# A feed-forward whose gate and up projections use seven block products for each eight, two batches at a time

## What is computed

```python
def _L0_ffn_ref(h_shard, w_gate_up, w_down):          # INTER = 2048
    gate_up = jnp.einsum('bsh,oh->bso', h_shard, w_gate_up)
    gate, up = jnp.split(gate_up, 2, axis=-1)
    h = jax.nn.silu(gate) * up
    return jnp.einsum('bsi,hi->bsh', h, w_down)
...
x = x + _L0_attn_a_ref(_layernorm(x, axis=-1), ...)
x = x + _L0_ffn_ref(_layernorm(x, axis=-1), L0_ffn_w_gate_up, L0_ffn_w_down)
x = x + _L0_attn_b_ref(_layernorm(x, axis=-1), ...)
x = x + _L0_ffn_ref(_layernorm(x, axis=-1), L0_ffn_w_gate_up, L0_ffn_w_down)
```

## Time and profile before

| | us |
|---|---|
| median of 3 runs | 3209.04 (3207.11 to 3210.09) |
| the profiled execution, whole | 3208.35 |
| its span, first to last instruction | 3207.1 |
| TensorE busy in the span | 3056.9 (95%) |
| VectorE, ScalarE, GpSimd busy | 2126.6, 1530.9, 584.5 |
| granted TensorE clock, mean of the span | 0.978 of full speed |

### The profile page before, as it was taken

How to read it: one execution, slowest core, us unless ns; L and a number is a source line. 1 busy time by engine, 2 the same in 40 slices (tenths; PEclk the granted TensorE clock), 3 DMA queues, 4 the chain that set the end, 5 groups by cost and what they waited for, 6 DMA issues and landing times.

```text
span 3207.1 us, 44240 instructions
## 1 busy us (share of the span) xinstructions
PE 3056.9 (95%) x17041; PEld 1739.5 (54%) x17041; DVE 2126.6 (66%) x4092; ACT 1530.9 (48%) x2483; POOL 584.5 (18%) x429
## 2 busy tenths in 40 slices
PE   6999999999999799999799999989899888999999
PEld 3434334334333344444488888854344336888887
DVE  6998998998989777776444334446676766444343
ACT  4988888888888366666511111014343342111110
POOL 1000000000000445442100001004454451001000
PEclk9999999999999799999899999999999988999999
DMA  2000000000000000000110000043232312001001
GB/s 74 2 1 11 1 1 11 1 1 11 1 1 2 1 2 1 2 1 2 59 40 20 20 20 1 1 131 86 66 99 79 86 34 79 20 20 40 1 1 53
DMA packets 32855, 86.96 MB, mean 27 GB/s; under 512 B 7235, under 2 KB 7236, under 8 KB 30469
## 3 DMA queue, kind: packets, MB, share of 16 engines
q1 hardware_dynamic: 30022, 83.43, 8.8%
q10 hardware_dynamic: 2624, 0.69, 0.1%
HBM read 59.60 MB, written 20.97 MB: 25 GB/s over the span
## 4 chain that ended last, share of the span: by engine, by line
PE 43%; DVE 3%; DMA 2%; POOL 2%; issue 1%; ACT 1%; SPq 0%; ACTq 0%; POOLq 0%; DVEq 0%
PE ps L1201 22%; PE ps L1215 11%; PE ps L1578 3%; POOL ex_sum L1546 2%; PE ps L1642 1%; PE ps L1608 1%; PE ps L1566 1%; PE ps L1619 1%; PE ps L1593 1%; DMA k_stack<-halves 1%; DMA halves<-lo_b 1%; DVE out_t L1706 1%; DVE ffn_z L1227 1%; PE ps L1186 1%; DVE sums_sb L1705 0%
## 5 line engine op out<-in xcount | busy, mean ns | idle before, releaser
L655 DVE TENSOR_SCALAR pair_in<-key_words,row_words 128x512 f32<-128x512 f32 x1792 | 726.1, 480 | 44.2 <-PE ps L542 40.2
L740 ACT ACTIVATE pair_mid<-ps,row_bias 128x512 f32<-128x512 f32 x896 | 588.2, 688 | 133.2 <-PE ps L542 115.8
L542 PE MATMUL ps<-pair_in,w_hi 128*64 128x512 f16 x3584 | 584.3, 390 | 8.6 <-DVE pair_in L655 8.2
L1278 ACT ACTIVATE ffn_silu<-ps 128x512 f32<-128x512 f32 x128 | 76.2, 595 | 831.4 <-PE ps L1201 831.4
L1240 DVE TENSOR_TENSOR ffn_inner<-ffn_silu,ps 128x512 f32<-128x512 f32 x128 | 87.9, 687 | 550.5 <-PE ps L1201 550.5
L542 PEld LDWEIGHTS ps<-pair_in,w_hi 128*64 128x64 f16 x3584 | 202.2, 108 | 301.6 <-issue 66.8
L1003 DVE TENSOR_REDUCE maxes<-ps 128x2 f32<-128x1024 f32 x256 | 303.1, 1221 | 93.6 <-PE ps L919 92.5
L542 PE MATMUL ps<-pair_in,w_lo 128*64 128x512 f16 x1792 | 352.1, 388 | 0.0
L1047 ACT ACTIVATE ex<-ps 128x512 f32<-128x512 f32 x448 | 243.2, 595 | 118.9 <-PE ps L938 118.4
L1201 PE MATMUL ps<-ffn_z_hi,ffn_w_hi 128*128 128x512 f32 x1024 | 277.4, 393 | 1.7 <-ACT ffn_w_hi L1267 1.7
L1201 PE MATMUL ps<-ffn_z_hi,ffn_w_lo 128*128 128x512 f32 x1024 | 274.7, 390 | 1.9 <-POOL ffn_w_lo L1285 1.9
(11 more groups left out here) (209 smaller groups left out, 4420.0 us busy)
## 6 DMA issues: line engine op xcount, KB each, us to landing
ffn_raw<-in_w_ffn SPq DMA_DIRECT2D x14, 1536.0 KB, 6.7
q_stack<-halves SPq DMA_DIRECT2D x48, 256.0 KB, 5.1
k_stack<-halves SPq DMA_DIRECT2D x48, 256.0 KB, 5.9
halves<-hi_b SPq DMA_DIRECT2D x16, 512.0 KB, 2.6
halves<-lo_b SPq DMA_DIRECT2D x16, 512.0 KB, 3.6
out<-x SPq DMA_DIRECT2D x4, 1024.0 KB, 4.3
x<-in_x SPq DMA_DIRECT2D x6, 512.0 KB, 5.9
ffn_raw<-in_w_ffn SPq DMA_DIRECT2D x6, 512.0 KB, 4.7
```

The costliest lines, as they stand in the source:

```text
L542: s = nc.tensor.matmul(ps[F2 * half:F2 * half + F2, bank + which, :], w_part[:, :], words.rearrange("p (s two) -> p s two", two=2)[:, :, o ...
L655: s = nc.vector.tensor_scalar(p.pair_in[:, (4 * n + i) % N_PAIR, :], p.key_words[:, b % 2, :], p.row_words[:, b % 2, row:row + 1], None, A ...
L740: nc.scalar.activation(p.pair_mid[:, n % NG, which, :], ps[:, bank + which, :], ACT.Relu, bias=bias).then_inc(p.mid_made, 1)
```

## The change

Write the weights of one block `o` as a 2 x 2 matrix of blocks: gate or up, by the first or second half of the 512 input features. Write the turned rows of two batches as another: first or second half of the features, by batch. Their product is four results: gate and up of the first batch (called low) and of the second (high). Done block by block it takes eight products of blocks; the change does it in seven, of sums and differences of blocks, and adds the seven up into the four results.

The loop runs over units `s` = 0 to 31 (`UNITS_F`): a pair of batches (16 units each) and a block. A unit has seven `product` steps of 6 matmuls (2 feature blocks x 3 passes), in the order 1, 6, 5, 2, 7, 3, 4 after the first unit, into three banks X (products 1, 2), Y (6, 7, 4) and Z (5, 3), with a second set of banks for the next unit. ScalarE copies bank X after product 1 into `first` and bank Z after product 5 into `fifth`, since products 2 and 3 then add onto these banks. VectorE makes `second` (after 6), `third` (after 7), the high gate (after 3) and the low up value (after 4), and both products with the silu; GpSimd makes the high up value, `third` + `fifth`. The copy into `in_hi` moves from VectorE to ScalarE.

The weights of a unit are 256 KB of down weights and 512 KB of gate and up weights in runs of 512 bytes, by two DMAs; each is loaded twice, once for each pair of batches. GpSimd makes four sums and differences of them (`sums`); ScalarE and GpSimd split seven blocks of weights where four were split. The seven operands of the other side are made once for each pair of batches (`difference`, `operand`). `down` now runs for both batches and both blocks at once, in every second unit: 24 matmuls after product 2 and 24 after product 3 of units 2, 4, 6, ..., and 48 after the last unit. There are 7 x 6 matmuls in a unit where two batches took 8 x 6.

```diff
+PAIRS = B // 2
+UNITS_F = PAIRS * NI
+A_PLACE = {1: 0, 2: 1, 4: 2, 5: 3, 6: 4, 7: 5, 3: 6}
+PRODUCTS = (1, 6, 5, 2, 7, 3, 4)
+FIRST_PRODUCTS = (1, 2, 5, 3, 6, 7, 4)
+LOW_BY_POOL = (3, 4)
...
 def order_of_feed_forward():
 
-    order = [("load", 0), ("load", 1), ("norm", 0), ("turned", 0, 0), ("turned", 0, 1), ("split", 0, 0),
...
+    for s in range(1, UNITS_F):
+        side = [[], []]
+        if s == 1:
+            side = [[("turned", 2, f) for f in range(ND)] + [("norm", 3)], [("turned", 3, f) for f in range(ND)]]
+        elif s % 2 == 0:
...
+        next_split = s + 1 < UNITS_F
+        order += [("product", s, 1), ("first_copy", s)] + after.get(1, []) + [("sums", s + 1)] * next_split
+        order += [("product", s, 6), ("second_sum", s)] + after.get(6, [])
+        order += [("product", s, 5), ("fifth_copy", s)] + after.get(5, [])
+        order += [("split", s + 1, part) for part in range(2)] * next_split
+        order += [("product", s, 2), ("gate_low", s)] + after.get(2, []) + side[0]
+        order += [("product", s, 7), ("third_sum", s)] + after.get(7, [])
+        order += [("product", s, 3), ("gate_high", s), ("up_high", s)] + after.get(3, [])
+        order += [("split", s + 1, 2)] * next_split + [("split_down", s)] + [("load", s + 2)] * (s + 2 < UNITS_F)
+        order += side[1] + [("inner_high", s), ("low_high", s), ("product", s, 4), ("up_low", s), ("inner_low", s),
+                            ("low_low", s)] + after.get(4, [])
+    return order + [("down", UNITS_F // 2 - 1, b, t) for b in (1, 0) for t in range(NT)]
 
 
...
+            elif kind == "product":
+                s, n = at
...
+                bank = bank_x(s) if n in (1, 2) else bank_y(s) if n in (6, 7, 4) else bank_z(s)
+                if n == 1:
+                    pe.wait_ge(gate_low_made, s - 1)
+                elif n == 6:
...
+                elif n == 2:
+                    pe.wait_ge(first_made, s + 1)
...
+                part = 0 if n in (1, 2) else 1 if n == 4 else 2
+                opens = n in (1, 6, 5)
+                place = n - 1
+                for m, (b_part, a_part) in enumerate(((b_hi, a_hi), (b_lo, a_hi), (b_hi, a_lo))):
+                    if m == 0:
+                        pe.wait_ge(w_hi_made, 3 * s + part + 1)
+                        pe.wait_ge(operand_hi, hi_of(p, n))
+                    elif m == 1:
+                        wait_for_low(pe, p, n)
+                    else:
+                        pe.wait_ge(w_lo_made, 3 * s + part + 1)
+                    for h in range(2):
...
+            elif kind == "operand" and at[1] not in LOW_BY_POOL:
+                p, n = at
+                dve.wait_ge(operand_hi, hi_of(p, n))
+                nc.vector.tensor_tensor(b_lo[:, n - 1], operand_of[n], b_hi[:, n - 1].bitcast(F32),
+                                        ALU.subtract).then_inc(lo_by_dve, 1)
+            elif kind == "second_sum":
+                s, = at
+                dve.wait_ge(product_done, products_to(s, 6))
+                dve.wait_ge(first_made, s + 1)
+                nc.vector.tensor_tensor(second[:, :], first[:, :], bank_y(s), ALU.add).then_inc(second_made, 1)
...
+            elif kind == "gate_high":
+                s, = at
+                dve.wait_ge(product_done, products_to(s, 3))
+                dve.wait_ge(second_made, s + 1)
+                dve.wait_ge(in_hi_made, 2 * s)
+                nc.vector.tensor_tensor(gate_1[:, :], second[:, :], bank_z(s), ALU.add).then_inc(gate_sum_made, 1)
+            elif kind == "inner_high":
+                s, = at
+                dve.wait_ge(gate_high_made, s + 1)
+                dve.wait_ge(up_high_made, s + 1)
+                nc.vector.tensor_tensor(gate_1[:, :], gate_1[:, :], up_1[:, :], ALU.mult).then_inc(inner_high_made, 1)
+            elif kind == "up_low":
+                s, = at
+                dve.wait_ge(product_done, products_to(s, 4))
+                dve.wait_ge(in_hi_made, 2 * s)
+                nc.vector.tensor_tensor(up_0[:, :], first[:, :], bank_y(s), ALU.add).then_inc(up_low_made, 1)
+            elif kind == "inner_low":
+                s, = at
+                dve.wait_ge(gate_low_made, s + 1)
+                dve.wait_ge(up_low_made, s + 1)
+                nc.vector.tensor_tensor(up_0[:, :], gate_0[:, :], up_0[:, :], ALU.mult).then_inc(inner_low_made, 1)
...
         def scalar(kind, *at):
             if kind == "split":
-                c, part = at
-                w, (first, end) = c % 2, PARTS[part]
-                if c == 0:
-                    act.wait_ge(first_loaded[part], 16)
+                s, part = at
+                source, hi, _ = parts_of(s, part)
+                if part == 2:
+                    act.wait_ge(sums_made, 4 * s + 4)
                 else:
-                    act.wait_ge(loaded[w], 16 * ((c + 1) // 2))
-                act.wait_ge(down_done, NT * B * (c - 1))
...
+            elif kind == "operand":
+                p, n = at
+                if n in differences_before:
...
+                    act.wait_ge(product_done, products_to(NI * p - 1, n))
+                nc.scalar.activation(b_hi[:, n - 1], operand_of[n], ACT.Copy).then_inc(operand_hi, 1)
+            elif kind == "first_copy":
+                s, = at
+                act.wait_ge(product_done, products_to(s, 1))
+                act.wait_ge(up_low_made, s)
+                nc.scalar.activation(first[:, :], bank_x(s), ACT.Copy).then_inc(first_made, 1)
...
+            elif kind == "gate_high":
+                s, = at
+                act.wait_ge(gate_sum_made, s + 1)
+                nc.scalar.activation(gate_1[:, :], gate_1[:, :], ACT.Silu).then_inc(gate_high_made, 1)
+            elif kind in ("inner_high", "inner_low"):
+                s, = at
+                b, inner = (1, gate_1) if kind == "inner_high" else (0, up_0)
+                act.wait_ge(inner_high_made if b else inner_low_made, s + 1)
+                act.wait_ge(down_done, 2 * NT * (s // 2))
+                nc.scalar.activation(in_hi[:, b, s % 2, :], inner[:, :], ACT.Copy).then_inc(in_hi_made, 1)
 
...
         def gpsimd(kind, *at):
-            if kind == "split":
-                c, part = at
-                w, (first, end) = c % 2, PARTS[part]
-                pool.wait_ge(w_hi_made, 3 * c + part + 1)
-                nc.gpsimd.tensor_tensor(w_lo[:, w, first:end], raw[:, w, first:end],
-                                        w_hi[:, w, first:end].bitcast(F32), ALU.subtract).then_inc(w_lo_made, 1)
+            if kind == "sums":
+                s, = at
+                i = s % 2
+                gate, up = raw_up[:, i, :, 0, :], raw_up[:, i, :, 1, :]
+                pool.wait_ge(loaded[i], 32 * (s // 2 + 1))
+                pool.wait_ge(w_hi_made, 3 * s)
+                nc.gpsimd.tensor_tensor(sums[:, 0], up[:, 0:2], up[:, 2:4], ALU.add).then_inc(sums_made, 1)
+                nc.gpsimd.tensor_tensor(sums[:, 2], gate[:, 0:2], up[:, 0:2], ALU.subtract).then_inc(sums_made, 1)
+                pool.wait_ge(sums_made, 4 * s + 2)
+                nc.gpsimd.tensor_tensor(sums[:, 1], sums[:, 0], gate[:, 0:2], ALU.subtract).then_inc(sums_made, 1)
+                pool.wait_ge(sums_made, 4 * s + 3)
+                nc.gpsimd.tensor_tensor(sums[:, 3], gate[:, 2:4], sums[:, 1], ALU.subtract).then_inc(sums_made, 1)
+                pool.wait_ge(sums_made, 4 * s + 4)
+            elif kind == "split":
+                s, part = at
+                source, hi, lo = parts_of(s, part)
+                pool.wait_ge(w_hi_made, 3 * s + part + 1)
+                nc.gpsimd.tensor_tensor(lo, source, hi.bitcast(F32), ALU.subtract).then_inc(w_lo_made, 1)
...
+            elif kind == "up_high":
+                s, = at
+                pool.wait_ge(third_made, s + 1)
+                pool.wait_ge(fifth_made, s + 1)
+                pool.wait_ge(inner_high_made, s)
+                nc.gpsimd.tensor_tensor(up_1[:, :], third[:, :], fifth[:, :], ALU.add).then_inc(up_high_made, 1)
...
             if kind == "load":
-                c, = at
...
+                s, = at
+                c, o = s % NI // OC, s % OC
+                sp.wait_ge(w_lo_made, 3 * (s - 1))
+                sp.wait_ge(down_lo_made, s - 1)
+                up = d["w_ffn"][c][:, 0:WU].rearrange("p (f g o n) -> p f g o n", f=ND, g=2, o=OC)
+                nc.sync.dma_start(raw_up[:, s % 2], up[:, :, :, o, :]).then_inc(loaded[s % 2], 16)
+                nc.sync.dma_start(raw_down[:, s % 2, :], d["w_ffn"][c][:, WU + o * D:WU + o * D + D]).then_inc(
+                    loaded[s % 2], 16)
```

More of the change, by code:

```diff
@@ L1145, in feed_forward @@
 def feed_forward(k, name, stored):
     nc, d, ps, x = k.nc, k.d, k.ps, k.x
[L1147 to L1149 removed]
+    pe, dve, act, pool, sp = (Since(queue, k.ffn_before) for queue in (k.pe, k.dve, k.act, k.pool, k.sp))
+    WU = ND * 2 * OC * P
     out_dram = d["out"].rearrange("b (t p) n -> b p t n", p=P)
     def signal(part):
[L1153 removed]
+        if part not in k.ffn_flags:
```

(12 more changed lines are left out.)

325 lines of the change are left out of this document (217 added, 108 removed).

## The result

The changed kernel takes **3324.18 us** (median of 4 runs, 3320.55 to 3334.3) against 3209.57 (median of 4 as well): a ratio of 1.0365, 95% interval 1.0352 to 1.0378, 114.6 us slower. The forecast was 3344. The profiled execution took 3319.3.

A forecast was written before the change was run, and what follows sets the result against it. TensorE's matmuls were taken to bound the kernel before. Fewer matmuls -87, waits in pairs +171, starts +32, change of batches +12, ends +7 give +135 on 3208.35, so 3343, median 3344 us; range 3262 to 3425.

The forecast's parts named there:

- Each step of the odd unit: Queues worked off: load lands at 5.0 us, TensorE loses 2.0 at product 6 and 3.45 at product 2.
- Rival (a): VectorE and GpSimd don't hold each other up: 2.65 us lost in a pair, time 3253; chance 0.17 with middle forms.
- (c): Small-block sums cost GpSimd less and the load lands early, so both waits of a pair vanish: 3181; chance 0.08.
- first norm to `first` of unit 2: Start of a feed-forward: unit 1 runs as if begun at 36.1 us; 3 more lost round turns of batches 2 and 3.
- 14 pairs of units: Ordinary pairs inside a feed-forward: each predicted to take 35.6 us against 32.64 before.
- extra of the change of batches: At unit 15 seven operands are made anew within a unit: 6 us (3 to 12) per feed-forward, +12 in all.
- the loss in a pair: TensorE's waits in two units: 0.25 + 2.0 + 3.45 = 5.7 us, in 30 pairs +171.
- The other outcome, VectorE first: VectorE wins the race with GpSimd's long split at 11.5 us of an odd unit: the pair comes to 34.9.
- GpSimd's 3.6 us before: GpSimd's work in a unit, put at 9.8 us after the change where it had 3.6.
- the weight traffic: Doubled weight loads called small beside 16 GB/s; DMAs held to be hidden but for the load's landing.
- The rival on the load: Part of a rival with chance 0.20: load lands at 7 instead of 5, moving the pair by 2: +60, 3404.
- The clock: Part of the same 0.20 rival: low clock after 30 waits of 3.45 us, 1.6 lost each: +48, 3392.

The follow-up runs named there:

- psum_inner: The changed kernel with gate_1, its silu, up_0 and both inner products kept in place in their PSUM banks; 3262.1 us against 3324.2.
- early_psum: psum_inner with the up-weights also loaded apart from the down-weights and issued a unit earlier; 3249.9 us against 3324.2 for the changed kernel.

## Why the prediction was right

**Sign and mechanism.** Each step of the odd unit is in the trace: the load lands late, the sums follow, `up_1` meets the silu, VectorE and GpSimd hold each other up, product 6 waits for `a_lo` and product 2 for `first`. The early load, the order and the PSUM edits moved what they should. Rival (a), no mutual hold-up, falls by L1401's 2.90 us and by psum_inner; (c) by the pair of 34.2.

**The sizes**, for one feed-forward (the first), predicted by the prediction's steps and measured. The total, first norm to last add, is 543.3 + 135/2 = 610.8 predicted and 598.3 measured (2167.70 + 0.69 - 1570.14).

| part | predicted | measured |
|---|---|---|
| first norm to `first` of unit 2 | 36.1 + 3 + 32 turns of 0.13 + 18.55 = 61.8 | 64.3 |
| 14 pairs of units | 14 x 35.6 = 498.4 | 14 x 34.1 = 477.4 |
| extra of the change of batches | 6 | 80.4 - 2 x 34.1 = 12.2 |
| the rest, to the total | 44.6 | 44.4 |

**The step that was too large** is the loss in a pair, 5.7 against 4.3. I count it from the starts of TensorE's matmuls, where two take 0.46 us and the first two behind a wait 0.1 more; the idle times of the trace come out 0.3 shorter, since the ends of matmuls are modelled. In the outcome that was priced, GpSimd first, product 6 lost 1.5 us (1797.29 to 1799.11) where 2.0 was put, and product 2 lost 2.9 (1800.60 to 1803.91) where 3.45 was. The first follows from the load: its landing was put at 5.5 us behind the issue and the sums start 4.8 behind it (1718.07 and 1722.90). For the second, `in_lo` behind the high product took 1.01 us and not 1.35. The other outcome, VectorE first, was priced at 34.9 and called about the same. It is the usual one (17 of 26 even units) and takes 33.5 to 33.8: product 6 lost 1.9 there (1730.11 to 1732.37), product 2 only 1.5 (1733.86 to 1735.76). The steps behind the 34.9 were not written down, so which of them was off, beyond the landing, stays open. **Too small** is the change of batches, at the far end of its 3 to 12; its waits (4.26 us for `third`, 2.36 for `a_lo`, the lower clock behind both) were not worked off beforehand. The errors have opposite signs, -21 and +6, and 2.5 for the start. So that the total came within 20 us is in part luck; the pair alone, -42 in two feed-forwards, would have left it in the range.

**Two readings were wrong and cost nothing.** GpSimd's 3.6 us before are for the weights of one block, which then served all four batches; for two batches they are 1.8, against 9.8. And the weight traffic, called small beside 16 GB/s, is 48 GB/s in the stretch where it was 16, the DMA share 0.16 instead of 0.05. No run traces a loss to it beyond the landing: in early_psum the earlier transfer cost nothing.

**The rival on the load** had a sooner or later load move the pair one to one. A load issued sooner gained nothing in this order, so that half is wrong. The other half isn't decided: 3.9 us of hold a pair gave 3.7, the clock included. **The clock** was held for possible, not likely, and is there in part. In the stretch with 0.93 most of it lies behind the waits of the change of batches; in the ordinary pairs it is four of nine waits of 2.7 us. Behind one of these, eight matmuls took 3.5 us and not 1.95 (1803.91 and 1735.76), so four of them are some 6 us (an estimate), not the 48 of the rival. It wasn't tested by itself.

**Of what would show it**: the waits and their places were right, L1401's mean is over 1 us but L1411's is 0.82, and the busy share was put at 80 to 85% and is 92% in ordinary pairs, 86% where the change of batches is in the stretch.

## What to carry to other kernels

Fewer matmuls pay only if every other queue keeps up: lay the queues of one period side by side by hand before you trust busy shares, since here GpSimd at 61% and VectorE at 53% of a stretch stopped TensorE for 8% of it. Leave intermediate results in their PSUM bank where the bank is free anyway, so that VectorE doesn't read two SBUF operands beside GpSimd. Waits that share a chain neither add nor can be judged one at a time: a step that costs alone may pay once its neighbours are mended.

## What the runs showed of the hardware

- A hold-up goes both ways and lasts to the end of the other's instruction: VectorE's 0.69 us became up to 2.90, GpSimd's 2.4 became 2.83 in a pair and up to 3.33 at a feed-forward's start.
- VectorE with one operand and the result in PSUM, in place, takes 693 to 696 ns, as into SBUF, and was never held up here (697 at most in 128 instances).
- Of two instructions that start almost together, the earlier one had the access, by 0.08 us at 1729.40 (VectorE) and by 0.03 at 1796.68 (GpSimd). This changes from pair to pair, so the period itself varies: mostly 33.5 to 33.8 us with VectorE first, 34.6 and more with GpSimd first, 35.0 to 36.2 where the lower clock fell into the pair.
- A wait of 2.7 us of TensorE is followed by the lower clock level in some cases (four of nine, granted clock 0.50) and not in others; none of seventeen of 1.3 us was.
